# A graph attention kernel whose gathers state the last row of their table as a bound

## The reference, cut to what matters

```python
h = jnp.maximum(_layernorm(x, axis=-1), 0.0)
q = (h @ Wq.T + bq); k = (edge_attr @ Wk.T + bk); v = (h @ Wv.T + bv)   # in 8 heads of 16
qs, qd = (q[src], q[dst])
in_m, out_m, diag_m = sum(qs * k), sum(qd * k), sum(qs * qd)            # over the 16 of a head
score = (segsoftmax(in_m * SCALE, dst) + segsoftmax(out_m * SCALE, dst)
         + segsoftmax(diag_m * SCALE, dst)) * distance ** lam
z = segment_sum(score[..., None] * v[dst], dst) @ Wo.T + bo
return x + leaky_relu(z, 0.1)
```

## Time and profile before

| | |
|---|---|
| median of 3 runs | 2371.37 us |
| span of the profiled execution | 2370.1 us |
| mean granted TensorE clock | 0.881 |
| gathers of `fetch_sources` | 1,664, mean 956 ns, first start 72.7 us, last start 2196.7 us |
| gathers of `fetch_results` | 98, mean 946 ns, first start 2232.3 us, last start 2353.6 us |
| busy share PE, DVE, POOL, ACT | 76%, 77%, 71%, 39% |

### The profile page before, as it was taken

One profiled execution on the slowest core, in us unless ns is written; L12 is line 12 of the kernel. 1 busy time (PEld: TensorE's weight loads), 2 busy tenths in 40 slices (PEclk: granted clock), 3 DMA queues, 4 the chain that ended last, 5 costly groups with the idle time before them and its releaser, 6 DMA issues. The chain is left out here.

```text
span 2370.1 us, 38721 instructions
## 1 busy us (share of the span) xinstructions
PE 1790.9 (76%) x11148; PEld 1099.0 (46%) x11148; DVE 1819.8 (77%) x3163; ACT 917.9 (39%) x1931; POOL 1694.6 (71%) x1775
## 2 busy tenths in 40 slices
PE   5568778887877787778777777787778787777377
PEld 4534444454444444444444444444444444444155
DVE  7569877787877778787777787877778787778556
ACT  8124434443444344434334334444434343343112
POOL 0647777777777777777777777777777777777375
PEclk9789988888999889999989898989988988898677
DMA  6788877776777777777776777777777777774345
GB/s 229 225 280 259 263 222 223 219 231 212 232 227 231 226 230 231 228 227 229 229 225 211 225 237 217 236 226 223 229 219 233 224 232 227 229 229 121 110 146 170
DMA packets 392243, 522.72 MB, mean 221 GB/s; under 512 B 80797, under 2 KB 300321, under 8 KB 378722
## 3 DMA queue, kind: packets, MB, share of 16 engines
q1 hardware_dynamic: 299922, 228.18, 32.1%
q10 hardware_dynamic: 35664, 179.21, 21.3%
q0 software_dynamic: 56448, 112.85, 17.9%
HBM read 435.41 MB, written 84.57 MB: 219 GB/s over the span
## 5 line engine op out<-in xcount | busy, mean ns | idle before, releaser
L135 POOL DMA_INDIRECT qsrc<-q_tab,idx_sb x1664 | 1590.9, 956 | 541.6 <-issue 525.8
L806 PE MATMUL qd_ps<-onehot,window 128*128 128x128 f32 x3328 | 527.2, 309 | 136.7 <-DVE onehot L1019 128.1
L912 ACT COPY kq<-qd_ps 128x512 f32<-128x512 f32 x416 | 242.7, 583 | 883.7 <-PE qd_ps L806 865.5
L806 PEld LDWEIGHTS qd_ps<-onehot,window 128*128 128x128 f32 x3328 | 475.0, 220 | 209.6 <-issue 200.1
L815 PE MATMUL qs_ps<-ident,qsrc 128*128 128x128 f32 x1664 | 282.4, 297 | 311.4 <-DMA qsrc<-q_tab,idx_sb 311.0
L1033 DVE TENSOR_TENSOR prod<-qs_ps,kq 128x1024 f32<-128x1024 f32 x416 | 506.1, 1217 | 3.7 <-PE qs_ps L815 2.5
L795 PE MATMUL k_ps<-ea_sb,wk_sb 128*128 128x512 f32 x832 | 491.1, 676 | 11.3 <-DMA ea_sb<-in_ea 11.3
L1029 DVE SCALAR_TENSOR_TENSOR prod<-k_ps,bk_col,kq 128x512 f32<-128x512 f32 x416 | 310.1, 746 | 114.0 <-PE lg_ps L785 99.2
L815 PEld LDWEIGHTS qs_ps<-ident,qsrc 128*128 128x128 f32 x1664 | 203.3, 151 | 396.8 <-issue 386.1
L785 PE MATMUL lg_ps<-prod,heads 128*32 128x384 f32 x3328 | 365.4, 512 | 1.1 <-DVE prod L1033 1.1
L906 ACT ACTIVATE kq<-k_ps,bk_col 128x512 f32<-128x512 f32 x416 | 285.6, 687 | 206.4 <-PE k_ps L795 205.2
(11 more groups left out here) (170 smaller groups left out, 1161.5 us busy)
## 6 DMA issues: line engine op xcount, KB each, us to landing
ea_sb<-in_ea ACTq DMA_DIRECT2D x104, 1024.0 KB, 6.2
window<-q_tab SPq DMA_DIRECT2D x1664, 64.0 KB
state<-rows ACTq DMA_DIRECT2D x104, 576.0 KB
near_sb<-near_tab SPq DMA_DIRECT2D x104, 512.0 KB
pa_sb<-pa_tab SPq DMA_DIRECT2D x104, 258.0 KB, 7.9
qsrc<-q_tab,idx_sb POOLq DMA_INDIRECT x1664
xs<-in_x SPq DMA_DIRECT2D x15, 448.0 KB, 5.6
q_tab<-qs SPq DMA_DIRECT2D x14, 448.0 KB, 2.5
```

Of the source, the lines that this page charges most:

```text
L135: pool.indirect_dma_start(out=qsrc[:, r, j, :], out_offset=None, in_=q_tab, in_offset=bass.IndirectOffsetOnAxis(ap=idx_sb[:, q, g * GRP + ...
L806: t = nc.tensor.matmul(qd_ps[:, at], window[:, r, j, :], onehot[:, m % 2, at], start=True, stop=True)
L912: nc.scalar.copy(kq[:, m % 2, 1, :], qd_ps[:, :]).then_inc(qd_copied, 1)
```

## The change

```diff
@@ def fetch_sources(pool, q, g)
                 pool.indirect_dma_start(out=qsrc[:, r, j, :], out_offset=None, in_=q_tab,
                                         in_offset=bass.IndirectOffsetOnAxis(
-                                            ap=idx_sb[:, q, g * GRP + j:g * GRP + j + 1], axis=0)
-                                        ).then_inc(q_in[r], 16)
+                                            ap=idx_sb[:, q, g * GRP + j:g * GRP + j + 1], axis=0),
+                                        bounds_check=NPAD + P - 1, oob_is_err=False).then_inc(q_in[r], 16)
@@ def fetch_results(pool, k)
                 pool.indirect_dma_start(out=st[:, k % RST, j, :], out_offset=None, in_=state,
-                                        in_offset=bass.IndirectOffsetOnAxis(ap=last_i[:, at:at + 1], axis=0)
-                                        ).then_inc(st_in[k % RST], 16)
+                                        in_offset=bass.IndirectOffsetOnAxis(ap=last_i[:, at:at + 1], axis=0),
+                                        bounds_check=EPAD - 1, oob_is_err=False).then_inc(st_in[k % RST], 16)
```

## The result

The changed kernel takes 2464.43 us, the median of 4 runs (2463.03 to 2467.16), beside 2371.66 us of the kernel before (2371.07 to 2372.61). The ratio is 1.0398, with a 95% interval from 1.0383 to 1.0413: 92.8 us more. The forecast was 2372 us in a range from 2325 to 2590 us, with 45% for slower. So the range holds the time, and the likeliest case was the wrong one. The rival "slower, by the form of the instruction", priced at 52 ns a gather and 2461 us, is what came.

What follows compares the result with a forecast made beforehand. The prediction took POOL's back-to-back gathers to bound the kernel: 2371.4 us plus 1,716 times the time added per gather. Its three parts summed to 0 + 0 + 0, with a longer instruction list 2372 us, range 2325 to 2590 us.

Steps and rivals of the forecast that it cites:

- slower, by the form of the instruction: Rival: register operand and compare lengthen each POOL gather by some tens of ns; at 52 ns 2461 us; chance 22%.
- What bounds the kernel: POOL's back-to-back gathers are the clock of edge and out pass: one every 1.25 us, 0.94 busy and 0.30 idle.
- The exposure of 1,716: Gathers on the path: 1,632 of the edge pass behind the first 32, 84 of the out pass; 1.7 us per ns.
- First part, the register write at 0: 1,762 register writes on POOL, one ahead of each gather, priced at 0 as covered by the 0.30 us gap.
- The argument from equal gaps with and without a semaphore: POOL's gaps between gathers are 0.30 or 0.31 us even with semaphore work, so a register write has room there.
- Second part, the bound at 0: Each gather's compare of 128 indices with the bound, taken as 0 because the error flag may already imply a comparison.
- The middle value, 52 ns: Middle price of the bound: scatter L766 takes 994 against gather L762's 942 ns on the same indices; +89 us.
- no change: Likeliest single case: the change adds nothing to POOL's gathers; 2372 us, own range 2367 to 2376 us; chance 35%.
- The rivals that pay for each index: Slower gathers: sequential check 123 ns, 2582 us, 12%; branches 411 ns, 3077 us, 3%; skill estimate 1.28 us, some 4570 us.
- Third part: Skipping and report: all indices are in range, so no row is skipped and POOL's queue moves the same 56,448 packets.
- the rival with 20%: Faster, since gathers no longer look for an error: -52 ns each, 2282 us; chance 20%.
- The signs: Profile marks: gather's 0.94 or 0.30 us grows, equally for both tables; TensorE's qsrc waits move about 1,632x; packets stay 56,448.

Runs made afterwards that it cites:

- experiment 1: The changed kernel with its bounds kept but the error flag left set on the gathers: 2491.35 us, ratio to the kernel before 1.0506.
- experiment 11: The kernel before with 32 of 128 indices in each edge-pass gather, plus the change's bounds: 2326.18 us in one run.
- experiment 2: The kernel before with only the error flag taken away from the 1,762 gathers, no bound stated: 2369.02 us, ratio 1.0003.
- experiment 3: The changed kernel with its two bounds written once to two registers at the program's start, not ahead of each gather: 2462.34 us, ratio 1.0392.
- experiment 4: The kernel before with four unused semaphore counts added ahead of each edge-pass gather: 2369.94 us in one run, beside 2369.32 us.
- experiment 5: The changed kernel without its first hunk, so the bound is only on the 98 gathers of the out pass: 2376.83 us, ratio 1.0028.
- experiment 6: The kernel before with the bound on the first of every four edge-pass gathers, none in the out pass: 2405.86 us, ratio 1.0135.
- experiment 8: The kernel before with each edge-pass gather cut to 64 of its 128 indices, no bound: 2303.29 us, ratio 0.9700.
- experiment 10: The kernel before with each edge-pass gather cut to 32 of its 128 indices, no bound: 2243.98 us in one run.
- experiment 12: The changed kernel with the edge-pass gathers' bound set to N // 2, so 49.9% of the edges' rows are skipped: 2464.88 us, ratio 1.0381.
- experiment 7: The kernel before with the bound on the first two of every four edge-pass gathers: 2438.53 us in one run.

## Why the prediction was right or wrong, point by point

- **The forecast as a whole.** Slower had the largest share, 45%, and the range of 2325 to 2590 us holds 2464 us. It holds it by its width: the sum itself gave 2372 us and missed by 92 us.
- **What bounds the kernel: right.** The edge pass follows POOL's gathers. Over gather times from 867 to 1011 ns the time follows 1,632 gathers of the edge pass and 84 of the out pass to within 7 us. From the median of the kernel before in the same batch, 64 indices give 2371.0 - 1,632 x 0.041 = 2304.1 us, and 2303.3 were measured; 32 indices give 2369.3 - 1,632 x 0.077 = 2243.7, and 2244.0 were measured; the change gives 2371.7 + 1,716 x 0.053 = 2462.6, and 2464.4 were measured. Experiments 1 and 11 came out above it: 2370.1 + 1,716 x 0.067 = 2485.0 and 2491.4 measured, 2369.3 - 1,632 x 0.032 + 84 x 0.053 = 2321.6 and 2326.2 measured. In both profiled executions the stretch from the start of the out pass's 84th gather to the end is 39.9 us in place of 34.0.
- **The exposure of 1,716: right to a dozen gathers.** The first 32 gathers were hidden: the 33rd starts at 142.20 us, before at 142.41 us. The gap behind them shrank from 27.38 to 25.37 us, where 32 x 0.053 = 1.7 was due, but that sign is too weak to be read. With gathers of 944 ns it is shorter still in experiment 2:

```profile
140.33 0.94 POOL L135 DMA_INDIRECT qsrc<-q_tab,idx_sb  x1 [24.70 <-issue]
```

  The chain of the changed kernel leaves POOL (2427.03 - 2318.68)/1.301 = 83 periods behind the first gather of L144, as before. (The prediction calls 2336.09 us a landing. It is the start of the 84th gather, whose piece of 5.22 us ends at 2341.3 us; the count of 84 stands.) In other executions the chain leaves at the 91st gather (experiment 1: (2458.65 - 2340.0)/1.315 = 90 periods) or at the 96th (experiment 2), which is worth 12 x 0.053 = 0.6 us at most.
- **First part, the register write at 0: right in its number, wrong in its cover.** It isn't the 0.30 us gap that hides it. The list writes the bound some 13 gathers ahead, and even 6,656 more instructions were free (experiments 3 and 4). The argument from equal gaps with and without a semaphore fitted both, and it rested on a wrong premise: the counts don't lie in those gaps, as L752 shows under experiment 4. That row would also have been a nearer price for the write, 17 ns, than the 83 ns of VectorE's accumulator; the write itself takes 29 ns.
- **Second part, the bound at 0: wrong, and this is the step that failed.** I took the end "it may vanish", on the guess that an error flag means that a comparison is made anyway. Experiment 2 shows that the flag without a bound changes nothing, and experiment 1 that it costs 14 ns as soon as a bound stands beside it, so the flag was no evidence of a comparison. In the place of 0 the stated bound costs 53 ns (experiment 3 rules out the register write, 4 a longer list and 5 a cause in the edge pass). Whether the comparison takes them or the handing over of the operand isn't shown. The middle value, 52 ns from the scatter of L766 beside the gather of L762, met it to 1 ns. That is luck. Each kernel has one such pair, which no edit touched, and its difference isn't steady: 959 and 1030 ns in the changed kernel, 942 and 1015 in experiment 6, and in experiment 8, which states no bound at all (there L762 and L766 are L766 and L770):

```profile
L770 POOL DMA_INDIRECT state<-fixed,fix_i x1 | 1.0, 1002 | 9.0 <-DVE fixed L1238 9.0
L766 POOL DMA_INDIRECT fix<-state,fix_i x1 | 1.0, 961 | 20.3 <-DMA state<-rows 20.3
```

  So it goes from 41 to 73 ns. What the pair was good for is the size: two forms of this instruction differ by tens of ns. With 3 ns as the least that can be measured, that spoke more for "slower by form" than for "no change", and seen from here the chances of 22% and 35% had it the wrong way round.
- **The compare was sized by index: wrong in its reasoning.** "It is work per index and fixed work" left open how much of each, and the range's upper end of 123 ns rested on the former. At 32 indices 867 of 944 ns remain, and the bound costs 45 ns instead of 13. The rivals that pay for each index, 123 and 411 ns and the estimate of 1.28 us, are out at 53 ns.
- **Third part: right.** No row was skipped and nothing got lighter: POOL's queue moved 112.85 MB as before. The sign that the prediction names, fewer packets, couldn't have shown it, since the packets stay at 56,448 whatever the rows (experiments 8, 10 and 12). That the readiness to report might have cost something before, the rival with 20%, is out by experiment 2.
- **The signs.** The period told everything, 0.94 grew and 0.30 stayed, and both tables have the same 53 ns, as the forecast asked. TensorE's waits for `qsrc` grew by 42 us only, from 311.0 to 353.0 us, and not by 1,632 x 0.053 = 87 us. TensorE was busy for 36.9 us longer and waited 12.8 us longer for VectorE's one-hot (128.1 us before); the three together are 91.7 us, beside the 91.1 us of the span. The wait table of the changed kernel:

```profile
ACT kq L912 <- PE qd_ps L806: 961.8, 242, 9.0
...
PE qs_ps L815 <- DMA qsrc<-q_tab,idx_sb: 353.0, 119, 5.8
DVE found L1116 <- PE t_ps L827: 223.0, 72, 5.3
...
PE qd_ps L806 <- DVE onehot L1019: 140.9, 81, 3.7
```

  ScalarE's wait for qd grew from 865.5 to 961.8 us, and VectorE's for the marks (L1116) from 160.4 to 223.0 us. TensorE's instructions stand in a fixed order, so a later gather also delays what stands behind `turn`, and idle time lands on whoever waits for that; this reading is argued from the kernel, not tested.
- **The rule weighed ahead of the result**, the Trainium skill, "DMA: Bandwidth & Descriptors", section "Anatomy of one DMA — SWDGE (gpsimd) path", by which the generation of descriptors is a small part beside the completion: by it the change would have cost nothing. The runs disagree for gathers issued back to back. 53 ns more in which a gather holds POOL were 92.8 us of the whole: the next gather comes after 0.94 + 0.30 us, while one landing takes 5.22 us, so landings overlap and don't set the pace.

## What to carry to other kernels

When one engine issues its DMAs back to back without a wait, the period of one issue times their number is the stage's time as long as the other engines keep up (here down to a period of 1.17 us, experiment 10), and an option on that instruction is priced in nanoseconds times the count: here 1,716, so that 3 ns would be 5 us, and 53 ns were 4%. State no bound where the indices are known to be in range; where a bound is needed, skipping silently was 14 ns a gather cheaper than reporting. And an error flag that stands in an instruction isn't evidence that a check is made: ask for what the check compares with.

## What the runs showed of the hardware that I had not expected

- POOL's instruction list runs ahead of its gathers, by 17.4 us at the last one. Register writes and semaphore counts between gathers are free, up to four a gather as far as tried.
- A gather of 128 rows holds POOL for 944 ns, one of 64 rows for 903 and one of 32 rows for 867 ns, each with 0.30 us behind it. At a quarter of the rows nine tenths of the time remain.
- Bounded and unbounded gathers in one stream cost each other up to 14 ns (experiments 6 and 7). The single unbounded gather of L762 takes 942 ns before and 959 ns behind the bounded stream of the changed kernel. It takes 961 ns behind a stream of 64 indices without a bound too (experiment 8), so a stated bound isn't needed for that. The cause is open.
- TensorE's granted clock, averaged over the span, was 0.899 with the 32-index gathers, 0.890 with 64, 0.881 in the kernel before and 0.863 in the changed one, while its waits for rows were 243, 276, 311 and 353 us. That is a tendency and no rule: with 32 indices and the bound the clock was 0.879 at 266 us of waits, and executions of the kernel before lie between 0.870 and 0.888. The mean of the changed kernel's matmuls in L806 was 316 ns instead of 309; the 91.1 us of the span are accounted for without it.
- A gather makes 32 packets in POOL's queue whether it fetches 128, 64 or 32 rows or skips half of them; only the bytes follow the rows (112.85, 58.33, 31.06 and 59.02 MB).
